# Normalising chunks for the next stage inside the routed-expert stage, a two-part zone router, and key-half sums on GpSimd

## The reference, cut to what matters

```
x = x + 0.5 * L0_ffn(layernorm(x))    # f0: 8 experts of 176, top 2, and a shared expert of 352
x = x + L0_attn(layernorm(x))         # a0: 16 heads of 8, 4 key heads
x = x + 0.5 * L0_ffn(layernorm(x))    # f0 again
x = x + 0.5 * L1_ffn(layernorm(x))    # f1: 8 zones of 128x512x128, top 3 for each batch row
x = x + L1_attn(layernorm(x))         # a1: 8 heads, latent keys of 32 and a shared rotary part
x = x + 0.5 * L1_ffn(layernorm(x))    # f1 again
```

## Time and profile before

| | before |
|---|---|
| median of 3 runs | 1517.97 us (1517.54 to 1518.09) |
| the profiled execution | 1523.39 us, of which the span from first to last instruction is 1521.4 us |
| busy in the span | PE 96%, DVE 72%, ACT 63%, POOL 38% |
| mean granted TensorE clock | 0.987 |
| stages, start of the first product loop in the span | f0 57, a0 318, f0 670, f1 959, a1 about 1117, f1 about 1366 |

### The profile page before, as it was taken

One profiled execution on the slowest core, in us unless ns is written; L12 is line 12 of the kernel. 1 busy time (PEld: TensorE's weight loads), 2 busy tenths in 40 slices (PEclk: granted clock), 3 DMA queues, 4 the chain that ended last, 5 costly groups with the idle time before them and its releaser, 6 DMA issues.

```text
span 1521.4 us, 27946 instructions
## 1 busy us (share of the span) xinstructions
PE 1457.4 (96%) x9950; PEld 1186.2 (78%) x9950; DVE 1099.7 (72%) x2377; ACT 958.2 (63%) x1710; POOL 581.7 (38%) x551
## 2 busy tenths in 40 slices
PE   6999999889999999999999999999979999989998
PEld 6788888775666665688888877899967777769998
DVE  3766766688888888476667665577768888866765
ACT  6455555447777777655555554777736666668886
POOL 4466566510000000026666653677710111136664
PEclk9999999999999999999999996999999999999999
DMA  6000000000000000000000003000000000000000
GB/s 176 1 1 1 1 0 2 1 0 2 1 1 1 1 2 1 1 1 1 2 0 1 1 26 143 1 2 2 2 1 2 1 2 2 2 2 2 15 15 29
DMA packets 13320, 16.88 MB, mean 11 GB/s; under 512 B 768, under 2 KB 10496, under 8 KB 12928
## 3 DMA queue, kind: packets, MB, share of 16 engines
q1 hardware_dynamic: 13184, 15.11, 3.2%
HBM read 13.01 MB, written 2.10 MB: 10 GB/s over the span
## 4 chain that ended last, share of the span: by engine, by line
PE 84%; DVE 8%; ACT 4%; issue 2%; DMA 1%; POOL 0%; DVEq 0%; SPq 0%; POOLq 0%; ACTq 0%
PE PS L604 20%; PE PS L632 10%; PE PS L1748 9%; PE PS L1761 8%; PE PS L741 5%; PE PS L761 5%; PE PS L749 4%; PE PS L1118 2%; PE PS L718 2%; PE PS L1093 2%; PE PS L1122 2%; PE PS L170 2%; PE PS L1075 1%; PE PS L1103 1%; PE PS L1142 1%
## 5 line engine op out<-in xcount | busy, mean ns | idle before, releaser
L542 POOL TENSOR_TENSOR RR<-AR,RR 128x512 fp32r<-128x512 f32 x150 | 193.9, 1293 | 490.7 <-ACT RR L565 490.7
L579 ACT ACTIVATE AR<-PS 128x512 f32<-128x512 f32 x224 | 134.0, 598 | 197.2 <-PE PS L604 196.0
L521 DVE TENSOR_TENSOR AR<-AR,PS 128x512 f32<-128x512 f32 x224 | 153.8, 687 | 132.3 <-PE PS L604 132.2
L859 ACT ACTIVATE AR<-PS 128x512 f32<-128x512 f32 x256 | 152.3, 603 | 85.9 <-PE PS L749 85.2
L932 DVE TENSOR_REDUCE AR<-PS 128x2 f32<-128x512 f32 x256 | 172.3, 686 | 21.5 <-PE PS L741 20.8
L604 PE MATMUL PS<-XHI,WG 128*128 128x512 f32 x448 | 175.7, 392 | 0.0
L604 PE MATMUL PS<-XHI,WU 128*128 128x512 f32 x448 | 174.6, 390 | 0.2
L525 DVE TENSOR_TENSOR AR<-AR,PS 128x512 f32<-128x512 f32 x224 | 153.9, 687 | 7.9 <-POOL RR L542 0.3
L1748 PE MATMUL PS<-XHI,SL 128*128 128x256 f32 x576 | 133.7, 287 | 2.6 <-DVE XTR L1914 1.5
L1748 PE MATMUL PS<-XLO,SL 128*128 128x256 f32 x576 | 133.0, 286 | 1.5 <-DVE XTR L1914 1.3
L741 PE MATMUL PS<-XLO,XHI 128*128 128x512 f32 x256 | 129.5, 506 | 3.0 <-DVE AR L932 2.4
(11 more groups left out here) (299 smaller groups left out, 3489.4 us busy)
## 6 DMA issues: line engine op xcount, KB each, us to landing
X<-in_x SPq DMA_DIRECT2D x4, 512.0 KB, 6.6
RAWZ<-in_zone_up SPq DMA_DIRECT2D x8, 256.0 KB, 5.0
RAWZ<-in_zone_down SPq DMA_DIRECT2D x8, 256.0 KB, 5.6
out_x<-X SPq DMA_DIRECT2D x4, 512.0 KB, 3.2
AR<-in_w SPq DMA_DIRECT2D x1, 1792.0 KB, 11.7
XT<-in_w SPq DMA_DIRECT2D x1, 1608.0 KB, 8.8
XT<-in_sel SPq DMA_DIRECT2D x1, 896.0 KB, 6.8
SM<-in_small SPq DMA_DIRECT2D x1, 857.5 KB, 7.2
```

Of the source, the lines that this page charges most:

```text
L521: v.tensor_tensor(PRD[:, m % 2, :], SIL[:, m % 2, :], bank(2 + m % 2), ALU.mult).then_inc(S.prod, 1)
L542: g.tensor_tensor(HL[k % 3], GAT[:, m % 2, :], HH[k % 3].bitcast(F32), ALU.subtract).then_inc(S.h_lo, 1)
L579: act.activation(SIL[:, m % 2, :], bank(m % 2), ACT.Silu).then_inc(S.silu, 1)
L859: act.activation(PT[:, g % 2, k, 2 * jp:2 * jp + 2, :], bank(2 + m % 2).rearrange("p (j q) -> p j q", j=2), ACT.Exp, scale=SC0).then_inc(S ...
```

## The change

1. **f0 normalises for the next stage.** After the statistics of chunk c-1 DVE aggregates them (`bn_aggr`), POOL raises to the power -0.5, DVE makes the bias, and in slots 10 to 13 ACT normalises the four tiles. In chunk c+1 PE transposes them (slot 0) and ACT copies (slot 2); before f1 DVE also makes the low part and the sum over tokens (slot 3). The tail of f0's chunks moves from slots 4 and 6 to 5 and 7. Only chunk 7 is left for the next stage's start, and the four phases `norm_*` and `f1_norm_*` are gone.
2. **Loads.** SP loads two zones and part A of a1's raw weights during f0, four zones after f0's last products, and the last two as slots come free. POOL now takes three low halves, DVE five.
3. **Router in two parts for the first f1 as well**: rows 0 to 9 inside f0's chunks 6 and 7, the other rows inside f1's loop (z = 11 to 24). The last f1 uses the same places, with 10 rows in the first part (8 before).
4. **a1.** POOL adds the two key halves of four heads' exponentials into PAIR; PE's sum over keys takes 4 matmuls for each half row of heads (8 before), in a function `sums` that stands one slot after `values`. `project_out`, `turn`, `next_turn`, `back`, `out_sums` and DVE's `add`, `stats`, `normalise`, `normed` move to later slots.

```diff
 def back(c):  # f0_dve
...
+                if ahead(n):
+                    v.wait_ge(S.st_new, D.st_new + c + 1)
+                    for k in range(c * TPC, (c + 1) * TPC):
+                        last = v.bn_aggr(MV[:, k, :], STAT[:, k, :])
+                    last.then_inc(N.ln, 1)
...
 def chunk(c, first):  # f0_dve
-                    if m == 6 and not first:
+                    if m == 7 and not first:
                         back(c - 1)
+                    if ahead(n) and m == 9 and not first:
+                        next_bias(c - 1)
+                    if to_zones(n) and m == 3 and c > 1:
+                        next_low(c - 2)
+                    if to_zones(n):
+                        early_route_dve(n + 1, MT0 * c + m, ROUTE_F0)
...
 f1_sp
-            sp.wait_ge(sem, count)
+            F, B = ST[n - 1], counts(n - 1)
+            sp.wait_ge(F.w_all, B.w_all + 1)
             for e in range(E1):
+                if e == 2:
+                    if n == PREP_IN:
+                        prep_sp(n + 1)
+                    sp.wait_ge(F.down, B.down + tiles0)
...
+                if e == 5:
+                    sp.wait_ge(F.back, B.back + NC)
...
 a1_pool
+            def pairs(b, half):
+                g.wait_ge(S.exp, NS1 * b + 4 * half + 4)
+                wait(g, S.av, 2 * b + half)
+                g.tensor_tensor(PAIR, PT[:, half, 0, :, :], PT[:, half, 1, :, :], ALU.add).then_inc(S.pair, 1)
...
 step of a1_pe
+                    if m == 0 and gone:
+                        project_out(i - 2)
+                    if m == 0 and done:
+                        turn(i - 1, 0)
                     if m == 1 and done:
                         values(i - 1, 1)
-                    if m == 3 and gone:
+                    if m == 2 and done:
+                        sums(i - 1, 1)
+                    if m == 4 and gone:
                         next_turn(i - 2)
-                    if m == 3 and done:
+                    if m == 4 and done:
                         turn(i - 1, 1)
...
-                    if m == 7 and now:
-                        turn(i, 0)
-                    if m == 7 and done:
-                        project_out(i - 1)
...
 step of a1_dve
+                    if m == 1 and gone:
+                        add(i - 2)
                     if 0 <= b < NB:
                         smax(b, s)
+                    if m == 1 and gone:
+                        stats(i - 2)
-                    if m == 0 and done:
+                    if m == 1 and done:
                         normalise(i - 1, 0)
...
-                    if m == 1 and gone:
+                    if m == 3 and gone:
                         normed(i - 2)
```

More of the change, by code:

```diff
@@ L224, in early, with ahead, bias_before @@
             return n + 1 < len(stages) and stages[n + 1] in ("a1", "f1") and stages[n] in ("f1", "a1")
+        def ahead(n):
+            return n + 1 < len(stages) and stages[n] == "f0"
         def normed_before(n):
-            return sum(runs[stages[j]] for j in range(n) if early(j))
+            return sum(runs[stages[j]] for j in range(n) if early(j) or ahead(j))
+        def bias_before(n):
+            return sum(runs[stages[j]] for j in range(n) if ahead(j))
         turned_before = normed_before
@@ L583, in chunk @@
                         high(c - 1, MT0 - 1)
+                    if ahead(n) and 10 <= m < 10 + TPC and not first:
+                        next_normed(c - 1, m - 10)
             for c in range(NC):
@@ L649, in chunk, with next_turn @@
                         down(c - 1, MT0 - 3 + m)
-                    if m == 4 and not first:
+                    if m == 5 and not first:
                         back(c - 1)
+                    if ahead(n) and m == 0 and c > 1:
+                        next_turn(c - 2)
+                    if to_zones(n):
+                        early_route_pe(n + 1, MT0 * c + m, ROUTE_F0)
+            def next_turn(c):
+                pe.wait_ge(N.xn, normed_before(n) + c + 1)
+                for t in range(TPC):
+                    last = pe.transpose(bank(7)[:, t * P:(t + 1) * P], XN[:, c % 2, t, :], ident)
+                last.then_inc(N.tr, 1)
             for c in range(NC):
@@ L655, in f0_pe @@
             down(NC - 1, MT0 - 3)
+            if ahead(n):
+                next_turn(NC - 2)
             down(NC - 1, MT0 - 2)
```

449 lines of the change are left out of this document (208 added, 241 removed).

## The result

The changed kernel took **1594.04 us** (median of 4 runs, 1592.25 to 1594.56), the kernel before 1518.03 us beside it: ratio 1.0488, 95% interval 1.0469 to 1.0507. The forecast was 1498.6 us and faster; the change costs 76 us.

What follows compares the result with a forecast made beforehand. PE alone was taken to bound f0's loop, a chain over all engines the gaps after it. Terms -15.3 - 29.0 + 6.2 + 2 + 1.7 + 5 + 10 = -19.4 us gave 1498.6 us, range 1474 to 1512.

Steps and rivals of the forecast that it cites:

- (d): a1: POOL's pair additions stop DVE, up to 2.36 us once a step, +33 us, 1531.6 us; chance 0.04.
- Term 6: a1: fewer matmuls with ones gain 0.86 us a step, new PE waits cost 0.8 and 1.1; +10 us.
- Term 3: f0's loop: PE's transposes of seven chunks, +6.2 us, and the router's DVE instructions waiting for POOL, +2 us.
- Term 1: Gap f0 to a0: only chunk 7's normalisation stays, so a0's first score comes earlier; -15.3 us.
- Term 2: Gap f0 to f1: f1 starts at 929.6 in place of 958.6; -29.0 us.
- Term 4: First f1's loop: table loads for the router's exp between gelus, plus small matmuls; +1.7 us.
- Term 5: Clock: PE at 1.2 GHz for some microseconds after each gap, bounds 0 and 11 us for both; +5 us.

Runs made afterwards that it cites:

- run 2: Changed kernel without POOL's pair additions in a1, PE summing with ones over both halves as before, new order kept: 1550.83 us, ratio 1.0215.
- run 7: Changed kernel with a1 as before, plus POOL's pair additions taken by the sums with ones, nothing moved: 1510.11 us, ratio 0.9937.
- run 6: Changed kernel with `normed` in slot 2 and DVE's low inputs, `vals`, stacks and slot 3's head keys moved ahead in a1: 1524.52 us, ratio 1.0029.
- run 8: Changed kernel with a1 as before; in f0 DVE's bias in slot 10 instead of 9, ACT's normalisations in slots 11 to 13: 1505.71 us, ratio 0.992.
- run 11: Changed kernel with a1 as before; POOL's bias additions in a0 start only after a0's first transposed score product: 1513.10 us, ratio 0.996.
- run 1: Changed kernel with `normed` in slot 2 of an a1 step instead of slot 3: 1542.02 us, ratio 1.0154.
- run 14: Kernel of run 6 with POOL's four low halves for the last f1 behind the pair additions of a1's last step: 1524.86 us, ratio 1.0034.

## Why the prediction was wrong

**Rival (d) was the case, at a chance of 0.04.** It named the mechanism, the victim (`normed`) and the place. The step that failed is the sentence against it: "by the walk the additions run 0.8 to 3.1 and 9.1 to 11.4 us into a step, beside instructions that read PSUM". The times in it were right. In the step shown, slot 0's score tile starts at 1216.59 and the additions at 1217.47 and 1225.97, so they run 0.9 to 3.2 and 9.4 to 11.7 us into the step. What was wrong is what stands beside them. `normed` starts at 1225.67, 9.1 us into the step, and it reads SBUF and writes SBUF. Term 6 itself had `normed` behind slot 3's maxima and ahead of the head keys, and used it for a wait of 0.5 us, but the prediction did not lay that place beside the addition's 9.1. The order alone says it too: `normed` stands behind the maxima of slot 3's score tile, and the fourth exponential, which releases the addition, comes from slot 3's transposed score tile, so the two meet in every step.

**(d) had the price of the lock right and two others missing.** It gave 2.36 us a step, +33 us in all. The lock itself cost 2.1 (2.73 less 0.59). The clock after it cost 1.5 us in most steps and 2.3 in four: the prediction had a clock term for the two gaps (5) and none for a1, and 11 of a1's 12 full steps fell to 1.2 GHz after or during the wait of 3.4 us. The third is the cost of the new order, see term 6. The rest of the way from (d)'s 1531.6 to 1594.0, 39 us, lies outside a1's loop, in terms 1 to 5 and in a1's end.

**Term 6, rest.** The waits were right: 0.8 expected for `vals`, 0.78 measured; 1.3 for the head keys, 1.24 (run 2). The gain of 0.86 a step was right as a price (0.85 in run 7), but the order in which the matmuls stand now costs 0.8 a step of its own, without any wait (run 6), and the term had that at nothing. The parts give the step: 14.5 + 1.9 for the waits + 0.8 for the order + 2.1 for the lock + 1.5 for the clock - 0.9 = 19.9 us. The term's last omission is a1's end, +10.6, for which the sum had no term.

**Term 3** was +6.2 and +2, and the two stretches grew by 24.8. 15.4 are 14 chunks of 1.10, of which 6.6 are the transposes as costed and 8.8 a stall (run 8). 7.6 are the router, 7.3 of them in the one chunk that took 37.9 us; the term had 2, and 6.5 at most. The rest is the later start. The prediction counted DVE's clump in slot 7 and gave it 2.6 us of tolerance. It did not count that DVE *waits* in slot 9 for POOL's power, which stands behind POOL's subtraction, two slots after the clump: what stands behind a wait on an engine's queue waits too.

**Term 1** (-15.3, measured -11.5): 3.0 of the missing 3.8 are the masks beside POOL's bias additions (run 11). **Term 2** (-29.0, measured -26.7) held. In the changed kernel ACT had rounded the last zone 14.0 us after X's last addition (14.5 expected), but from the instruction that was L1431 to the first product it took 11.2 us and not 8.3, since DVE's low halves, three of which took 2.02, 2.78 and 3.37 us beside POOL's, were then still under way, to 938.2. **Term 4** (+1.7): +5.3. In the first f1 PE waited 1.3 us at each of two places where it had not before (DVE's copy for a1, and DVE's maximum ahead of the router's exp); no run took it apart. **Term 5** (+5) lies in the gaps' measured sums and is not separable. The granted clock was 0.83 over 305 to 325, where it had been 1.00 before, and 0.86 over 919 to 955, where it had been 0.62; so only the first gap has more time at the lower clock than before.

The Trainium skill's rule that the prediction cited (SBUF — State Buffer, "Who interferes with whom") holds in the rows shown here. TENSOR_SCALAR and CAST from SBUF to SBUF and instructions with two SBUF inputs waited to the end of POOL's instruction. The CAST of the maxima, for one, takes 0.17 us in the changed kernel's step and 0.67 to 1.79 in run 1, where POOL's addition meets it (15 rows of 16). TENSOR_REDUCE (0.15 us at 1348.61) and the head keys with their one SBUF input (735 to 748 ns, all 64 in run 1, 28 of them beside the addition) never did. Nor did the same normalising instruction in the first f1, where its input lies in PSUM (0.40 to 0.41 us, all 32, 25 of them beside a copy of POOL's). The prediction quoted the rule and then did not ask which instruction stands at 9.1 us.

## What to carry to other kernels

When work is put on GpSimd, list every DVE instruction of the kinds named above that hangs on the same release as the new instruction, and treat each as a hit until the order keeps them a slot apart; the price is the longest single POOL instruction, so keep these short. In this kernel a wait of 3.4 us on a busy TensorE cost another 1.5 to 2.3 us through the clock in eleven of twelve steps. And cut work out in place: the same pair additions gave 0.85 us a step where nothing moved, and nothing where the moves of part 4 came with them, even with every wait gone.

## What was not expected of the hardware

Two groups of matmuls on 32-column tiles take 1.43 us side by side and 1.57 us with full-width matmuls between them (runs 7 and 6, start to start). The Trainium skill (TensorEngine Tiling (Array Packing), "Key Properties") says that changing the tiling mode drains TensorE; these rows agree, and put a number to it. And an instruction's own size says nothing of its price beside POOL: one of 10x8 took 1.99 us (run 14, 0.22 alone), as it waited for the rest of an addition of 2.37 us.
